# A recurrent step whose candidate's input v and candidate n lie in spare PSUM columns instead of SBUF

## The chip, the cores and the metric

One core of a Trainium2 chip runs the kernel. The time is that of one execution on the device, in microseconds (us); the profile is one execution taken by the hardware profiler. Engines: PE multiplies matrices (PEld is its weight load), DVE is the vector engine, ACT the scalar engine with tanh, POOL and SP have side roles here. SBUF is the working memory, PSUM the memory that PE writes its products to; DVE and ACT can read it, too.

## The reference

Four layers follow each other, each between two layer norms and added to its input x of 8 sequences, 512 tokens and 128 features. The first layer is a gated recurrent unit (GRU) with 256 hidden values, and only this one matters here. It goes through the 512 tokens one after the other:

```python
def step(h, xt):
    xr_t, xz_t, xn_t = xt
    r = jax.nn.sigmoid(xr_t + h @ w_hr.T + b_hr)
    z = jax.nn.sigmoid(xz_t + h @ w_hz.T + b_hz)
    n = jnp.tanh(xn_t + r * (h @ w_hn.T + b_hn))
    h_new = (1.0 - z) * n + z * h
    return (h_new, h_new)
```

The other three are a feed-forward layer with experts, an attention layer and a second feed-forward layer.

## The kernel before

The hidden state of all 8 sequences is kept turned: 128 partitions hold half of the 256 hidden values, and 16 columns (NSTEP) are the 2 halves times 8 sequences. So every elementwise operation of a step works on a tile of 128x16. For the matmuls the state is split into a high and a low fp16 part, the tile GB.

The 512 steps are written as 32 groups of 16 steps. The function `schedule` writes out, for each engine, the order: `steps` is the recurrent step itself, and between two steps `inputs`, `early`, `late` and `prepare` place pieces of other work (the layer norm of coming tokens, the output product of the GRU, the expert layer, weights for later stages). Each engine has one queue and takes its instructions in the order in which they are written; `wait_ge` on a semaphore holds the queue until another instruction has counted it up.

One step is, in the names of the code and the lines of the profile:

- PE (L731) multiplies the state by the recurrent weights, in the order r, part of n, rest of r, rest of n, z: 36 matmuls of 128x8. `r_ps`, `hn_tr` and `z_ps` are counted up as r, n and z are complete. Then it adds the input products and biases of the next four steps (`inject`, L739 and L744).
- ACT takes tanh of the r gate from PSUM: tr (L935).
- DVE makes u = (tr + 1) * hn with the product hn from PSUM (L1027), and v = u + xn with the input part xn from PSUM (L1031).
- ACT takes tanh of the z gate: tz (L937), and then tanh of v: n (L939).
- DVE makes zg = (tz + 1) * h (L1034), and zn = (tz - 1) * n (L1037). zg stands ahead of zn in DVE's queue.
- DVE makes the new state 0.5 * zg - zn, once as the high part in GB (L1041) and once in f32 in HR (L1042), and the low part as their difference (L1044). PE waits for the high part before the next step's first matmul, and for the low part a little later.

The sigmoids are written as tanh of half the argument, with factors folded into the weights.

PSUM has 8 banks of 512 f32 columns for each partition. Banks 0 and 1 belong to the r gate (pR), 2 and 3 to z (pZ), 4 and 5 to the candidate (pN), two banks each because four steps (U = 4) use bank p while the next four are prepared in bank 1 - p. In a pN bank the columns 0 to 63 hold hn and 64 to 127 hold xn of four steps; the columns from 128 on (2 * U * NSTEP) are not used. tr, tz, u_, v_, n_, zg and zn lie in SBUF.

Of the kernel before, what the change touches and what calls it, by code (L numbers as in the profile page):

```python
# [21 lines left out]
ALU = mybir.AluOpType  # L22
ACT = mybir.ActivationFunctionType
AX = mybir.AxisListType

P = 128
# [12 lines left out]
U = 4  # L39
NSTEP = HC * B  # L40
# [20 lines left out]
def build(nc, x_d, gamma_d, beta_d, w_ih_d, w_hh_d, b_ih_d, b_hh_d, w_out_d, b_out_d,  # L61
# [4 lines left out]
    with top:  # L66
        def sb(ctx, name, shape, dt=F32):
            return ctx.enter_context(nc.sbuf_tensor(name, shape, dt))
# [46 lines left out]
        def signal(name, per=1, credit=0):  # L115
            return Signal(top.enter_context(nc.semaphore(name)), per, credit)
# [83 lines left out]
        ctx = ExitStack()  # L200
# [251 lines left out]
        ctx = ExitStack()  # L452
        with ctx:
# [7 lines left out]
            tr = sb(ctx, "tr", [P, NSTEP])  # L461
            tz = sb(ctx, "tz", [P, NSTEP])
            u_ = sb(ctx, "u_", [P, NSTEP])
            v_ = sb(ctx, "v_", [P, NSTEP])
            n_ = sb(ctx, "n_", [P, NSTEP])
            zg = sb(ctx, "zg", [P, NSTEP])
            zn = sb(ctx, "zn", [P, NSTEP])
            warm = sb(ctx, "warm2", [P, 1])
            pR = PS[:, 0:2, :]
            pZ = PS[:, 2:4, :]  # L470
            pN = PS[:, 4:6, :]

            hr_start = signal("hr_start")
            x_stats = Signal(stats.sem, 1, 2)
# [23 lines left out]
            v_ready = signal("v_ready")  # L498
            n_ready = signal("n_ready")
            zg_ready = signal("zg_ready")  # L500
            zn_ready = signal("zn_ready")
# [419 lines left out]
            def _(act):  # L921
# [3 lines left out]
                n_scale = act.alloc_register("n_scale")  # L925
# [3 lines left out]
                def steps(first, s, ring):  # L929
                    p, k = s // U % 2, s % U  # L930
                    n = first + (s + 1) if isinstance(first, int) else act.snap(first + (s + 1))
                    now = lambda bank: bank[:, p, 0:U * NSTEP].rearrange("p (c u b) -> p c u b", c=HC, u=U)[:, :, k, :]
                    as_states = lambda x: x[:, :].rearrange("p (c b) -> p c b", c=HC)
                    act.wait_ge(r_ps.sem, n)
                    act.activation(as_states(tr), now(pR), ACT.Tanh, scale=gate_scale).then_inc(hn_tr.sem, 1)  # L935
                    act.wait_ge(z_ps.sem, n)
                    act.activation(as_states(tz), now(pZ), ACT.Tanh, scale=gate_scale).then_inc(tz_ready.sem, 1)  # L937
                    act.wait_ge(v_ready.sem, n)
                    act.activation(n_[:, :], v_[:, :], ACT.Tanh, scale=n_scale).then_inc(n_ready.sem, 1)  # L939

                def inputs(j, s):
                    if s == 0:
# [20 lines left out]
                def prepare(a):  # L963
# [38 lines left out]
                    if a == 7 * GS + 3:  # L1002
                        act.wait_ge(wsc.sem, wsc.value(act, 0, 8))
                        act.activation(WH[:, :], wguT[:, :], ACT.Copy, scale=W_UP).then_inc(wsplit.sem, 1)
                schedule(act, steps, inputs, early, late, prepare)

            @block.vector
            def _(dve):
# [8 lines left out]
                def steps(first, s, ring):  # L1017
                    p, k = s // U % 2, s % U
                    n = first + (s + 1) if isinstance(first, int) else dve.snap(first + (s + 1))
                    n2 = (first + (s + 1)) * 2 if isinstance(first, int) else dve.snap(first * 2 + 2 * (s + 1))  # L1020
                    by_chunk = lambda x: x.rearrange("p (c b) -> p c b", c=HC)
                    hn, xn = [pN[:, p, i * U * NSTEP:(i + 1) * U * NSTEP].rearrange("p (c u b) -> p c u b", c=HC, u=U)[:, :, k, :]
                              for i in range(2)]
                    before, now = HR[:, 1 - s % 2, :], HR[:, s % 2, :]

                    dve.wait_ge(hn_tr.sem, n2)
                    dve.scalar_tensor_tensor(by_chunk(u_[:, :]), by_chunk(tr[:, :]), 1.0, hn,  # L1027
                                             ALU.add, ALU.mult).then_inc(u_ready.sem, 1)

                    dve.wait_ge(u_ready.sem, n)  # L1030
                    dve.tensor_tensor(by_chunk(v_[:, :]), by_chunk(u_[:, :]), xn, ALU.add).then_inc(v_ready.sem, 1)  # L1031

                    dve.wait_ge(tz_ready.sem, n)
                    dve.scalar_tensor_tensor(zg[:, :], tz[:, :], 1.0, before, ALU.add, ALU.mult).then_inc(zg_ready.sem, 1)  # L1034

                    dve.wait_ge(n_ready.sem, n)
                    dve.scalar_tensor_tensor(zn[:, :], tz[:, :], 1.0, n_[:, :], ALU.subtract, ALU.mult).then_inc(zn_ready.sem, 1)  # L1037

                    dve.wait_ge(zn_ready.sem, n)
                    high, low = [GB[:, ring, i, :, s, :] for i in range(2)]  # L1040
                    dve.scalar_tensor_tensor(high, by_chunk(zg[:, :]), 0.5, by_chunk(zn[:, :]), ALU.mult, ALU.subtract).then_inc(g1_ready.sem, 1)  # L1041
                    dve.scalar_tensor_tensor(now, zg[:, :], 0.5, zn[:, :], ALU.mult, ALU.subtract).then_inc(g_ready.sem, 1)  # L1042
                    dve.wait_ge(g_ready.sem, n)
                    dve.tensor_tensor(low, by_chunk(now), high, ALU.subtract).then_inc(g2_ready.sem, 1)  # L1044
# [102 lines left out]
                def prepare(a):  # L1147
# [106 lines left out]
                    if a in (7 * GS + 5, 7 * GS + 10):  # L1254
                        half_w = slice(0, HID) if a == 7 * GS + 5 else slice(HID, 2 * HID)
                        dve.wait_ge(wsplit.sem, wsplit.value(dve, 0, 1))
                        dve.wait_ge(wsc.sem, wsc.value(dve, 0, 8))
                        dve.scalar_tensor_tensor(WL[:, half_w], wguT[:, half_w], W_UP, WH[:, half_w], ALU.mult, ALU.subtract).then_inc(wsplit.sem, 1)
                schedule(dve, steps, inputs, early, late, prepare)

        def layer_norm_scale(eng, mv, rt, rs, step, b, k):
# [23 lines left out]
        ctx = ExitStack()  # L1285
        with ctx:
# [61 lines left out]
            xn = signal("xn_ready", NT)  # L1348
# [1196 lines left out]
```

## Time and profile before

| | |
|---|---|
| median of 3 runs | 1646.24 us |
| the runs | 1638.33 to 1646.63 us |
| span of the profiled execution, first to last instruction | 1636.9 us |
| the profiled execution's own time with what lies around the span | not listed |
| the recurrence in it (25 to 1019 us) | 994 us |
| what follows (1019 to 1636.9 us) | 618 us |
| busy over the span: PE, DVE, ACT | 1365.0, 1143.2, 704.4 us |

A share of busy time tells little here. A step is a chain through three engines that repeats 512 times, so the thing to read is the order of time within one step: when each instruction starts, how long it takes, and which of its two inputs came last. An instruction of DVE or ACT is shown with its start and its duration; the time between the end of one and the start of the one that waits for it is the cost of handing over.

### The profile page before, as it was taken

What the parts mean: (1) busy time and instruction counts of PE and PEld (TensorE: products, weight loads), DVE (VectorE), ACT (ScalarE), POOL (GpSimd) and SP (SyncE); (2) the same over time, 40 slices, a digit from 0 to 9 for tenths busy, and PEclk for the clock granted to TensorE, in tenths of its full rate; (3) what the DMA queues carried; (4) which work ended last, traced back from release to release, by engine and by line L of the source; (5) the groups of instructions that cost most, each with busy time, mean ns of one, the idle gap of its engine ahead of it and who ended that gap; (6) DMA issues with size and microseconds to landing.
All of it is one profiled execution on the core that took longest, in us unless ns stands there. A gap on an engine that the chain in (4) does not pass through costs nothing. (4 is left out here: it accounts for less than half of the span.)

```text
span 1636.9 us, 65673 instructions
## 1 busy us (share of the span) xinstructions
PE 1365.0 (83%) x27355; PEld 1027.9 (63%) x27370; DVE 1143.2 (70%) x5594; ACT 704.4 (43%) x2475; POOL 434.8 (27%) x818
## 2 busy tenths in 40 slices
PE   5888888878878888888888887379999999999886
PEld 4667777767767777777777776245556555555443
DVE  5767777777777777777777776557576776776485
ACT  3333223222222222222222222136777777777765
POOL 2001111111111111111111111364245535522354
PEclk6555555555555555555555555578999999999998
DMA  5200000000000000000000000068537735742001
GB/s 120 29 4 5 5 7 5 5 6 5 5 5 7 5 5 6 5 5 7 5 5 7 5 5 7 7 140 139 73 66 110 98 58 89 106 68 29 1 14 39
DMA packets 68941, 53.70 MB, mean 33 GB/s; under 512 B 12686, under 2 KB 68390, under 8 KB 68646
## 3 DMA queue, kind: packets, MB, share of 16 engines
q1 hardware_dynamic: 66470, 49.32, 18.3%
q8 instruction: 215, 3.52, 0.9%
q14 instruction: 80, 0.66, 0.1%
q10 hardware_dynamic: 2176, 0.20, 0.1%
HBM read 31.84 MB, written 15.47 MB: 29 GB/s over the span
## 5 line engine op out<-in xcount | busy, mean ns | idle before, releaser
L731 PE MATMUL PS<-GB,W 128*128 128x8 f16 x18432 | 575.7, 168 | 177.3 <-DVE GB L1041 173.2
L731 PEld LDWEIGHTS PS<-GB,W 128*128 128x128 f16 x18432 | 532.6, 104 | 285.9 <-DVE GB L1041 281.1
L935 ACT ACTIVATE tr<-PS 128x16 f32<-128x16 f32 x512 | 94.7, 185 | 490.2 <-PE PS L731 490.2
L2383 DVE TENSOR_REDUCE MX<-PS 128x1 f32<-128x512 f32 (+3 forms) x352 | 220.0, 635 | 114.8 <-PE PS L1842 111.6
L2121 ACT ACTIVATE PT<-PS 128x512 f32<-128x512 f32 (+1 forms) x352 | 193.2, 566 | 114.7 <-PE PS L1858 110.1
L937 ACT ACTIVATE tz<-PS 128x16 f32<-128x16 f32 x512 | 94.2, 184 | 192.0 <-PE PS L731 192.0
L1027 DVE SCALAR_TENSOR_TENSOR u_<-tr,PS 128x16 f32<-128x16 f32 x512 | 87.4, 171 | 126.0 <-PE PS L731 114.0
L685 POOL TENSOR_TENSOR rt<-mv,eps 128x1 f32<-128x1 f32 x96 | 18.4, 191 | 553.1 <-DVE mv L1052 553.1
L1034 DVE SCALAR_TENSOR_TENSOR zg<-tz,HR 128x16 f32<-128x16 f32 x512 | 90.1, 176 | 81.5 <-ACT tz L937 81.4
L1839 PE MATMUL PS<-KS,QS 99*128 99x256 bf16 (+3 forms) x512 | 134.0, 314 | 12.8 <-DVE MX L2383 8.5
L1855 PE MATMUL PS<-QS,KS 102*128 102x256 bf16 (+3 forms) x512 | 128.8, 302 | 6.2 <-ACT PT L2121 5.6
L744 PE MATMUL PS<-Y,V 128*128 128x32 f16 x2322 | 130.9, 188 | 0.0
L739 PE MATMUL PS<-ones,brow 128*128 128x32 bf16 x1032 | 110.3, 188 | 2.1 <-PEq L201 2.1
L939 ACT ACTIVATE n_<-v_ 128x16 f32<-128x16 f32 x512 | 110.5, 216 | 0.4 <-DVE v_ L1031 0.2
L1044 DVE TENSOR_TENSOR GB<-HR,GB 128x16 f16<-128x16 f32 x512 | 89.5, 175 | 17.4
L1041 DVE SCALAR_TENSOR_TENSOR GB<-zg,zn 128x16 f16<-128x16 f32 x512 | 89.3, 174 | 17.6
L1031 DVE TENSOR_TENSOR v_<-u_,PS 128x16 f32<-128x16 f32 x512 | 87.1, 170 | 17.5
L744 PEld LDWEIGHTS PS<-Y,V 128*128 128x128 f16 x2322 | 98.7, 104 | 0.0
L1839 PEld LDWEIGHTS PS<-KS,QS 99*128 99x128 bf16 x512 | 45.0, 102 | 78.6 <-DVE MX L2383 37.4
L1037 DVE SCALAR_TENSOR_TENSOR zn<-tz,n_ 128x16 f32<-128x16 f32 x512 | 89.6, 175 | 0.6 <-ACT n_ L939 0.2
L1842 PE MATMUL PS<-maskU,identb 128*128 128x128 bf16 x512 | 89.5, 226 | 0.0
L1858 PE MATMUL PS<-maskL,identb 128*128 128x128 bf16 x512 | 86.9, 220 | 0.0
(393 smaller groups left out, 2496.8 us busy)
## 6 DMA issues: line engine op xcount, KB each, us to landing
QS<-q_parts SPq DMA_DIRECT2D x90, 128.0 KB, 11.0
KS<-k_parts SPq DMA_DIRECT2D x90, 128.0 KB, 13.1
q_parts<-PQ SPq DMA_DIRECT2D x16, 384.0 KB, 10.4
k_parts<-PK SPq DMA_DIRECT2D x16, 384.0 KB, 3.3
X<-XM SPq DMA_DIRECT2D x32, 64.0 KB
out_dram<-X SPq DMA_DIRECT2D x8, 256.0 KB, 2.3
XM<-in_L_attn_x_dram SPq DMA_DIRECT2D x16, 80.0 KB
s_hh<-in_L_attn_w_hh_dram SPq DMA_DIRECT2D x1, 768.0 KB, 5.4
```

The lines of the kernel that those rows point to most:

```text
L731: return pe.matmul(bank[:, p, at:at + B], W[:, kc, w:w + P], state[:, part, kc, :], start=False, stop=True, skip_group_check=True)
L739: pe.matmul(o, brow[:, (bias + mc) * P:(bias + mc + 1) * P], ones3[:, :], start=start and mc == 0, stop=False, skip_group_check=True)
L744: pe.matmul(o, V[:, w], Y[:, rows], start=False, stop=False, skip_group_check=True)
L935: act.activation(as_states(tr), now(pR), ACT.Tanh, scale=gate_scale).then_inc(hn_tr.sem, 1)
L937: act.activation(as_states(tz), now(pZ), ACT.Tanh, scale=gate_scale).then_inc(tz_ready.sem, 1)
L939: act.activation(n_[:, :], v_[:, :], ACT.Tanh, scale=n_scale).then_inc(n_ready.sem, 1)
L1034: dve.scalar_tensor_tensor(zg[:, :], tz[:, :], 1.0, before, ALU.add, ALU.mult).then_inc(zg_ready.sem, 1)
L1037: dve.scalar_tensor_tensor(zn[:, :], tz[:, :], 1.0, n_[:, :], ALU.subtract, ALU.mult).then_inc(zn_ready.sem, 1)
L1839: pe.matmul(bank[:, a * w:(a + 1) * w], QS[0:KM, p, 4 * g + i, q], KS[0:KM, p, 4 * g + i, 0:w], start=(a == 0), stop=False, skip_group_che ...
L1855: pe.matmul(bank[:, a * w:(a + 1) * w], KS[0:KF, p, 4 * g + i, j * P:(j + 1) * P], QS[0:KF, p, 4 * g + i, j * P:S], start=(a == 0), stop=F ...
L2121: act.activation(PT_OF[j][:, heads[0]:heads[-1] + 1, :], p_e[:, k % 2, 0:len(heads) * w].rearrange("p (a w) -> p a w", w=w), ACT.Exp).then ...
L2383: dve.tensor_reduce(MX[:, g % 2, heads[0]:heads[-1] + 1, NT - 1 - it], p_x[:, k % 2, 0:len(heads) * w].rearrange("p (a w) -> p a w", w=w), ...
```

## The change

v and n get new places. Instead of two SBUF tiles of 128x16 they are views of the candidate gate's own PSUM bank, the one of the current p: v in columns 128 to 143, n in columns 144 to 159. DVE writes v to PSUM (it already reads xn from the same bank), ACT reads v from PSUM and writes n to PSUM, and DVE reads n from PSUM for zn. No instruction, wait or semaphore is added, removed or moved.

```diff
-            v_ = sb(ctx, "v_", [P, NSTEP])
-            n_ = sb(ctx, "n_", [P, NSTEP])
...
+            def v_of(p):
+                return pN[:, p, 2 * U * NSTEP:2 * U * NSTEP + NSTEP]
+
+            def n_of(p):
+                return pN[:, p, 2 * U * NSTEP + NSTEP:2 * U * NSTEP + 2 * NSTEP]
...
-                    act.activation(n_[:, :], v_[:, :], ACT.Tanh, scale=n_scale).then_inc(n_ready.sem, 1)
+                    act.activation(n_of(p), v_of(p), ACT.Tanh, scale=n_scale).then_inc(n_ready.sem, 1)
...
-                    dve.tensor_tensor(by_chunk(v_[:, :]), by_chunk(u_[:, :]), xn, ALU.add).then_inc(v_ready.sem, 1)
+                    dve.tensor_tensor(by_chunk(v_of(p)), by_chunk(u_[:, :]), xn, ALU.add).then_inc(v_ready.sem, 1)
...
-                    dve.scalar_tensor_tensor(zn[:, :], tz[:, :], 1.0, n_[:, :], ALU.subtract, ALU.mult).then_inc(zn_ready.sem, 1)
+                    dve.scalar_tensor_tensor(zn[:, :], tz[:, :], 1.0, n_of(p), ALU.subtract, ALU.mult).then_inc(zn_ready.sem, 1)
```

## Rows read from the trace of the kernel before

**Rows 1.** Stage totals: stretch, length, busy us (instructions) per engine, PE clock, DMA.
```profile
25.00:1019.00 994.00, 816.15 (x22962) 705.15 (x22959) 723.65 (x4497) 297.78 (x1679) 157.42 (x364) 0.50 0.04 9
1019.00:1636.90 617.90, 540.58 (x4316) 316.04 (x4331) 406.82 (x1061) 399.37 (x785) 270.93 (x425) 0.92 0.43 69
```
**Rows 2.** Groups, 60 to 1090 us: busy us, mean ns | idle before, releasers.
```profile
L731 PE MATMUL PS<-GB,W 128*128 128x8 f16 x17776 | 555.2, 168 | 170.7 <-DVE GB L1041 166.7
...
L939 ACT ACTIVATE n_<-v_ 128x16 f32<-128x16 f32 x494 | 106.6, 216 | 0.4 <-DVE v_ L1031 0.2
...
L935 ACT ACTIVATE tr<-PS 128x16 f32<-128x16 f32 x494 | 91.4, 185 | 474.4 <-PE PS L731 474.4
L937 ACT ACTIVATE tz<-PS 128x16 f32<-128x16 f32 x494 | 90.9, 184 | 185.2 <-PE PS L731 185.2
...
L1037 DVE SCALAR_TENSOR_TENSOR zn<-tz,n_ 128x16 f32<-128x16 f32 x494 | 86.5, 175 | 0.6 <-ACT n_ L939 0.2
...
L1027 DVE SCALAR_TENSOR_TENSOR u_<-tr,PS 128x16 f32<-128x16 f32 x494 | 84.4, 171 | 118.5 <-PE PS L731 106.6
L1031 DVE TENSOR_TENSOR v_<-u_,PS 128x16 f32<-128x16 f32 x494 | 84.1, 170 | 16.9
```
**Rows 3.** Order of time, one step: start us, duration us, instruction [idle before, releaser].
```profile
600.37 0.18 ACT L935 ACTIVATE tr<-PS 128x16 f32<-128x16 f32 x1 [1.08 <-PE PS L731]
600.61 0.17 DVE L1027 SCALAR_TENSOR_TENSOR u_<-tr,PS 128x16 f32<-128x16 f32 x1 [0.17 <-PE PS L731]
...
600.82 0.17 DVE L1031 TENSOR_TENSOR v_<-u_,PS 128x16 f32<-128x16 f32 x1
...
600.93 0.18 ACT L937 ACTIVATE tz<-PS 128x16 f32<-128x16 f32 x1 [0.38 <-PE PS L731]
...
601.02 0.22 ACT L939 ACTIVATE n_<-v_ 128x16 f32<-128x16 f32 x1
...
601.15 0.18 DVE L1034 SCALAR_TENSOR_TENSOR zg<-tz,HR 128x16 f32<-128x16 f32 x1 [0.16 <-ACT tz L937]
601.27 0.18 DVE L1037 SCALAR_TENSOR_TENSOR zn<-tz,n_ 128x16 f32<-128x16 f32 x1
601.48 0.17 DVE L1041 SCALAR_TENSOR_TENSOR GB<-zg,zn 128x16 f16<-128x16 f32 x1
601.58 0.17 DVE L1042 SCALAR_TENSOR_TENSOR HR<-zg,zn 128x16 f32<-128x16 f32 x1
...
601.71 1.04 PE L731 MATMUL PS<-GB,W 128*128 128x8 f16 x33 [0.26 <-DVE GB L1041]
...
602.31 0.18 ACT L935 ACTIVATE tr<-PS 128x16 f32<-128x16 f32 x1 [1.07 <-PE PS L731]
```
**Rows 4.** Order of time on DVE, end of the last of the 155 steps.
```profile
899.91 0.17 DVE L1034 SCALAR_TENSOR_TENSOR zg<-tz,HR 128x16 f32<-128x16 f32 x1 [0.16 <-ACT tz L937]
900.03 0.17 DVE L1037 SCALAR_TENSOR_TENSOR zn<-tz,n_ 128x16 f32<-128x16 f32 x1
900.24 0.17 DVE L1041 SCALAR_TENSOR_TENSOR GB<-zg,zn 128x16 f16<-128x16 f32 x1
900.33 0.17 DVE L1042 SCALAR_TENSOR_TENSOR HR<-zg,zn 128x16 f32<-128x16 f32 x1
```
**Rows 5.** Order of time, a step in which DVE had other work before u.
```profile
255.57 0.17 DVE L1031 TENSOR_TENSOR v_<-u_,PS 128x16 f32<-128x16 f32 x1
255.74 0.18 DVE L1034 SCALAR_TENSOR_TENSOR zg<-tz,HR 128x16 f32<-128x16 f32 x1
255.78 0.21 ACT L939 ACTIVATE n_<-v_ 128x16 f32<-128x16 f32 x1
...
256.03 0.18 DVE L1037 SCALAR_TENSOR_TENSOR zn<-tz,n_ 128x16 f32<-128x16 f32 x1
```
**Rows 6.** Order of time on PE, a step with much other work.
```profile
605.20 0.31 PE L856 MATMUL PS<-DN,IL 128*128 128x128 f16 x1
...
605.59 0.27 PE L731 MATMUL PS<-GB,W 128*128 128x8 f16 x4
```

## The prediction

> **What bounds the kernel now.** I read the stage totals first, then the groups of instructions, then one recurrent step in order of time. The stage totals cut the span in two: 994 us of recurrence, 512 steps one after the other, and 618 us that the diff doesn't touch [rows 1]. Inside the recurrence PE is busy for 816 of the 994 us, DVE for 724 and ACT for 298: none is at its limit, so look for a chain of latencies. 994 / 512 is 1.94 us a step, and in the groups each link of the step has the same count [rows 2].
>
> The step in order of time gives the chain [rows 3]. Read from tr: tr starts at 600.37, u at 600.61, v at 600.82, n at 601.02, zn at 601.27, the state GB at 601.48. PE starts the next step's matmuls at 601.71, and the next tr starts at 602.31. The steps agree with each other to the last digit shown. I read the 155 steps between 600 and 900 us the same way; the first is that of [rows 3], the end of the last stands in [rows 4]. Their mean spacings are tr to u 0.241, u to v 0.207, v to n 0.203, n to zn 0.249, zn to GB 0.210, and from GB to the next tr 0.83: 1.94 us. So everything from v to zn is on the path today, and 1 ns taken from each step is 0.512 us of the kernel.
>
> A second branch runs beside it: PE finishes the z gate, ACT makes tz (600.93), DVE makes zg (601.15), and zg stands ahead of zn in DVE's queue. Two rows off the pattern show which branch releases zn. At 255 us a busy DVE made u and v late, with tz long done: n still follows v by 0.21 and zn follows n by 0.25, while zg was 0.29 ahead [rows 5]. So n releases zn. But in the usual step zg is only 0.12 ahead, and the only pair of SBUF operations here that run back to back, GB and HR, start 0.09 to 0.10 apart [rows 3, 4]. Over the 155 steps the means are 0.1206 and 0.0915: zn can move up by 0.029 us and no more, whatever happens to n. Then PE's z gate, ACT's tz and zg set the step.
>
> **The change part by part.** No instruction, wait, semaphore or DMA is added or taken away, and no queue is reordered. Three instructions per step change the memory of an operand: v (DVE) writes PSUM, n (ACT) reads and writes PSUM, zn (DVE) reads n from PSUM. u, tr, tz, zg, GB, HR and the low part stay.
>
> *n reads PSUM.* Same operation, same shape, same SBUF output: tr and tz read PSUM and take 185 and 184 ns, n reads SBUF and takes 216 [rows 2]. I take the whole difference: -31 ns.
>
> *zn reads PSUM.* By duration there is nothing to pay: u and v, with one PSUM input, take 171 and 170 ns, zn, all SBUF, 175 [rows 2]. By start after a wait on DVE's own result: v (reads PSUM) starts 0.207 - 0.171 = 0.036 after u's end, GB (reads SBUF) 0.210 - 0.175 = 0.035 after zn's end. That is +1 ns. A dearer reading exists: u starts 0.241 - 0.185 = 0.056 after tr's end, zg only 0.218 - 0.184 = 0.034 after tz's end, and u reads PSUM. If PSUM is the cause, zn pays +22 ns. The view of groups puts most of u's idle time down to PE (the hn product that u also needs), not to tr [rows 2], so I take +1 and keep +22 as the upper bound. Below, -5 (the difference of durations).
>
> *v writes PSUM; n writes PSUM.* No row of this trace has DVE or ACT writing PSUM. Both write 128x16 f32, as before. The largest difference between the two memories that any row shows for this size is the 31 ns above, so I bound each by -31 and +31. A saving on v would be worth little: n would then stand behind tz, which starts only 0.09 ahead of it [rows 3]. I take 0 for both: on DVE the nearest rows (PSUM reads) differ from SBUF by 5 ns at most; for ACT the only known sign is a gain, which the room at zg would swallow anyway.
>
> VectorE: DVE Perf Modes, a page of the Trainium skill, section "The TRN2 errata", speaks against this change: it gives VectorE 58 cycles of fixed cost from SBUF and 120 from PSUM at 0.96 GHz, and ScalarE 224 and 172 at 1.2 GHz. My estimate from that page would be +65 ns for zn and -43 for n, +22 a step, 11 us slower. This trace bears out the ScalarE half in sign (31 ns) and not the VectorE half (171 and 170 against 175).
>
> *What is hidden.* PE's other work, after the z gate, must be done by the time GB releases the next step. PE's idle time there is 170.7 us over 17776 matmuls, 36 to a step, so 0.35 us on average [rows 2]; in a tight step the filler's last matmul ends at 605.51 and the next step's first starts at 605.59 [rows 6], so 0.03 us less still fits. I counted 62 of 477 steps with under 0.11 us of it; should each of those lose 0.03, that is 2 us. DVE's side work lies between the low part and the next u, a stretch that starts with GB and doesn't shrink. While v and n are in use PE writes the z gate's banks and injects into the candidate's other bank (1 - p), so it has no need to wait for them.
>
> *The sum.* -31 (n's read) + 1 (zn's read) + 0 + 0 = -30 ns against a room of 29: -29 ns x 512 = -14.8 us. The profiled execution spans 1636.9 us; what lies around the span isn't shown, but it is 1.4 us under the fastest run (1638.3) and 9.3 under the median (1646.2). The saving is per step and holds for either; the runs shown themselves spread by 0.5%. From the median: 1646.2 - 14.8 = **1631.4 us**; from the span it would be 1622.1 plus what lies around it.
>
> **The rivals.**
>
> *VectorE pays for PSUM (slower).* DVE's write-back of v and its read of n are both dearer than to SBUF, by the two upper bounds: +31 and +22, less n's 31: +22 ns a step, +11.3 us, **1657.5 us**. It decides for slower (by 0.5%, 8.2 us, 16 ns a step) as soon as DVE's two PSUM accesses together cost more than 47 ns. For it: nothing here shows a DVE write to PSUM, and u starts late. Against it: the two DVE groups that read PSUM take no longer than the one that doesn't [rows 2]. The errata section of the Trainium skill's page VectorE: DVE Perf Modes, named above, comes out at nearly the same time.
>
> *One price only (no change).* Only zn's read costs 22: -9 ns, -4.6 us, 1641.6. Or only v's write costs 31: 0, 1646.2. Either eats the gain, and the edit is a wash. For it: u's late start. Against it: PE as the shown cause.
>
> *The room is smaller.* zn, reading PSUM, may not start 0.0915 behind zg but later; every 10 ns costs 5.1 us of the gain. The case of no change begins at 13 ns.
>
> *More than the room (faster).* Nothing on this path can give more than 29 ns unless PE runs faster. PE's granted clock is 0.50 (the 1.2 GHz level) through the recurrence and 0.92 after it [rows 1]; an idle stretch shorter by 0.03 of 0.35 us gives me no reason to expect another level. If it came, the z branch would shorten too.
>
> **How the numbers follow.** Forecast, with a gain of 16 to 29 ns: 0.55. More than that: 0.02. One price or a smaller room, within 8 us: 0.23. VectorE pays: 0.20. A difference of 0.5% (1638.0 or 1654.5 us) is about what a measurement of this kernel can tell from no change, so faster 0.57, same 0.23, slower 0.20. The unknown costs reach from -29 ns (1631.4) to +31 - 31 + 31 + 22 = +53 ns (+27.1 us, 1673.4). The forecast's own range is 1620 to 1638: the low end is the fastest run less 14.8, 1623.5, and a little for spread. The range of 8 in 10 runs from 1620 to 1659: it holds the case of no change and half of the slower one; what lies above, some 0.1, is v's write and n's write both dear.
>
> **What would show it.** Right: n, now PS<-PS, at about 185 ns or less; v at 170; zn starting about 0.09 after zg; DVE idle before zn no longer ended by n; a step of 1.91 us. Wrong: v well over 200 ns; zn starting later than 0.25 after n; a spacing zg to zn at 0.12 or more. If n falls to 185 and the step stays at 1.94, look at v's duration and at n's start after v first. The 618 us after the recurrence should be the same; if they differ, that isn't this change.

## The result, and the profile after

The changed kernel took 1626.0 us (median of 4 runs, 1624.6 to 1630.5) against 1646.4 (4 runs): a ratio of 0.9886, 95% interval 0.9862 to 0.991. By the ratio it is faster by 1.1%, 18.8 us of 1646.4 (the two medians lie 20.4 apart), where 14.8 were forecast. The profiled execution spans 1624.5 us.

The stage totals of the changed kernel, in the columns of [rows 1], cut at 1000 us, where the recurrence now ends:
```profile
25.00:1000.00 975.00, 816.51 (x22960) 705.45 (x22957) 709.27 (x4495) 277.26 (x1679) 155.32 (x364) 0.50 0.04 9
1000.00:1624.50 624.50, 546.30 (x4316) 321.68 (x4331) 407.26 (x1062) 399.23 (x785) 270.78 (x425) 0.92 0.43 68
```
The whole gain is in the recurrence. The exact cut is the first and the last tr of the 512 steps; this is the view of one line (duration shortest/median/longest, first and last start), for the kernel before:
```profile
L935 ACT ACTIVATE tr<-PS x512: 185/185/185, 24.9 to 1017.7; 128x16 f32<-128x16 f32 x171
```
and for the changed one, whose lines stand 4 lower from here on:
```profile
L939 ACT ACTIVATE tr<-PS x512: 183/183/183, 24.9 to 999.0; 128x16 f32<-128x16 f32 x171
```
992.8 us became 974.1: 18.7 us less, 37 ns for each of 511 steps. The usual step went from 1.94 to 1.90 us.

The groups of the changed kernel, as in [rows 2]:
```profile
L939 ACT ACTIVATE tr<-PS 128x16 f32<-128x16 f32 x494 | 90.4, 183 | 471.4 <-PE PS L735 471.3
L941 ACT ACTIVATE tz<-PS 128x16 f32<-128x16 f32 x494 | 90.4, 183 | 187.0 <-PE PS L735 187.0
L1035 DVE TENSOR_TENSOR PS<-u_,PS 128x16 f32<-128x16 f32 x494 | 88.1, 178 | 16.9
...
L1045 DVE SCALAR_TENSOR_TENSOR GB<-zg,zn 128x16 f16<-128x16 f32 x494 | 86.3, 175 | 16.8
...
L943 ACT ACTIVATE PS<-PS 128x16 f32<-128x16 f32 x494 | 83.0, 168 | 0.4 <-DVE PS L1035 0.2
L1041 DVE SCALAR_TENSOR_TENSOR zn<-tz,PS 128x16 f32<-128x16 f32 x494 | 81.2, 164 | 0.4 <-ACT PS L943 0.2
```
v (now `PS<-u_,PS`) went from 170 to 178 ns, n (`PS<-PS`) from 216 to 168, zn (`zn<-tz,PS`) from 175 to 164. Nothing else in the step changed by more than 2 ns.

One step of the changed kernel in order of time, to be laid beside [rows 3]:
```profile
601.39 0.18 ACT L939 ACTIVATE tr<-PS 128x16 f32<-128x16 f32 x1 [1.07 <-PE PS L735]
...
601.83 0.18 DVE L1035 TENSOR_TENSOR PS<-u_,PS 128x16 f32<-128x16 f32 x1
...
601.95 0.18 ACT L941 ACTIVATE tz<-PS 128x16 f32<-128x16 f32 x1 [0.38 <-PE PS L735]
...
602.04 0.17 ACT L943 ACTIVATE PS<-PS 128x16 f32<-128x16 f32 x1
602.16 0.18 DVE L1038 SCALAR_TENSOR_TENSOR zg<-tz,HR 128x16 f32<-128x16 f32 x1 [0.15 <-ACT tz L941]
602.25 0.16 DVE L1041 SCALAR_TENSOR_TENSOR zn<-tz,PS 128x16 f32<-128x16 f32 x1
602.45 0.17 DVE L1045 SCALAR_TENSOR_TENSOR GB<-zg,zn 128x16 f16<-128x16 f32 x1
602.54 0.17 DVE L1046 SCALAR_TENSOR_TENSOR HR<-zg,zn 128x16 f32<-128x16 f32 x1
602.68 0.81 PEld L735 LDWEIGHTS PS<-GB,W 128*128 128x128 f16 x27 [0.75 <-DVE GB L1045]
```
zn stands 0.09 behind zg, as HR stands behind GB: the two run back to back. Over 158 steps between 600 and 900 us, of which this is the first, the means, in the trace's own nanoseconds, are tr to v 0.445 us (0.446 before), v to n 0.213 (0.204), n to zn 0.209 (0.248), zg to zn 0.092 (0.121), zn to GB 0.198 (0.210). From tr to GB that is 1.066 us for 1.107. The rest, GB to the next tr, is 0.835 for 0.833.

### The profile page after: what moved, and what is told of

The parts are those of the page before. It is cut to its first block and busy times, and to the rows that moved or that the text cites. A ratio compares the mean times of both kernels' runs of the same rounds, so it can differ in the third digit from the quotient of the medians.

```text
span 1624.5 us, 65673 instructions
## 1 busy us (share of the span) xinstructions
PE 1371.2 (84%) x27355; PEld 1033.9 (64%) x27370; DVE 1129.3 (70%) x5594; ACT 683.8 (42%) x2475; POOL 432.6 (27%) x818
## 3 DMA queue, kind: packets, MB, share of 16 engines
q1 hardware_dynamic: 66470, 49.32, 18.8%
## 5 line engine op out<-in xcount | busy, mean ns | idle before, releaser
L1035 DVE TENSOR_TENSOR PS<-u_,PS 128x16 f32<-128x16 f32 x512 | 91.3, 178 | 17.5
L1048 DVE TENSOR_TENSOR GB<-HR,GB 128x16 f16<-128x16 f32 x512 | 90.2, 176 | 17.4
L1045 DVE SCALAR_TENSOR_TENSOR GB<-zg,zn 128x16 f16<-128x16 f32 x512 | 90.0, 176 | 17.4
L943 ACT ACTIVATE PS<-PS 128x16 f32<-128x16 f32 x512 | 86.0, 168 | 0.4 <-DVE PS L1035 0.2
L1046 DVE SCALAR_TENSOR_TENSOR HR<-zg,zn 128x16 f32<-128x16 f32 x512 | 86.1, 168 | 0.0
```

Source lines behind the costliest of these rows:

```text
L1035: dve.tensor_tensor(by_chunk(v_of(p)), by_chunk(u_[:, :]), xn, ALU.add).then_inc(v_ready.sem, 1)
```

## The experiments

The step times below are means over the steps between 590 and 910 us, the durations means between 600 and 900 us; "the 512 steps" are counted from the first tr to the last. The theory after the result: each operand's memory has a price of its own on the operation; n's prices are the large ones; and z's branch (PE, tz, zg) now sets zn's start, with n ready only a little earlier. Each edit is shown against the changed kernel, shortened.

**v alone in PSUM.**
```diff
-  act.activation(n_of(p), v_of(p), ...)
+  act.activation(n_[:, :], v_of(p), ...)
-  dve.scalar_tensor_tensor(zn[:, :], tz[:, :], 1.0, n_of(p), ...)
+  dve.scalar_tensor_tensor(zn[:, :], tz[:, :], 1.0, n_[:, :], ...)
```


> v in PSUM, n back in SBUF. Theory (each operand has its own price): v stays at 178 ns (170 in SBUF), n reads PSUM and writes SBUF and takes 185 as tr and tz do (216 before, 168 after), zn reads SBUF and takes 175 again. From tr, n ends at 0.844 us and zn starts 0.03 later at 0.876, which is 0.10 after zg, so n is still the later one. The step is 1.915 us (1.939 before, 1.900 after), 12 us of the 512 steps. Rival (n's 48 ns come from its write alone): n takes 216, v costs 8 more, the step is 1.948 us, 4 us slower than before.

Its groups:
```profile
L944 ACT ACTIVATE n_<-PS 128x16 f32<-128x16 f32 x157 | 28.9, 184 | 0.0
...
L1036 DVE TENSOR_TENSOR PS<-u_,PS 128x16 f32<-128x16 f32 x156 | 27.8, 179 | 5.3
...
L1042 DVE SCALAR_TENSOR_TENSOR zn<-tz,n_ 128x16 f32<-128x16 f32 x157 | 27.4, 174 | 0.0
```
The step is 1.917 us, the ratio 0.9945 (0.9929 to 0.996). The theory's numbers stand, the rival is out: reading v from PSUM takes 32 ns off n, writing v there adds 8 to v. zn starts 0.098 us after zg, so n releases it. Against the changed kernel the step is 16 ns longer, and most of that is two things: zn starts 7 ns later, and it takes 174 ns and not 164.

**n alone in PSUM.**
```diff
-  act.activation(n_of(p), v_of(p), ...)
+  act.activation(n_of(p), v_[:, :], ...)
-  dve.tensor_tensor(by_chunk(v_of(p)), ...)
+  dve.tensor_tensor(by_chunk(v_[:, :]), ...)
```


> n in PSUM, v back in SBUF. Theory (each operand has its own price): v takes 170, n reads SBUF and writes PSUM and takes about 200 (216 less the 16 that the write saves), zn reads PSUM and takes 164. zn starts 0.88 after tr, 0.105 after zg, and the state follows 0.198 later: a step of 1.912 us, 14 us less than before in the 512 steps. Rival (the write alone is what makes n short): n takes 168, zn stands 0.09 behind zg, the step is 1.900 as with both. Second rival (zn's shorter time has another cause than its PSUM input): zn takes 175.

Its groups:
```profile
L944 ACT ACTIVATE PS<-v_ 128x16 f32<-128x16 f32 x157 | 29.4, 187 | 0.0
...
L1042 DVE SCALAR_TENSOR_TENSOR zn<-tz,PS 128x16 f32<-128x16 f32 x157 | 26.8, 170 | 0.0
L1036 DVE TENSOR_TENSOR v_<-u_,PS 128x16 f32<-128x16 f32 x157 | 26.8, 170 | 5.4
```
The step is 1.908 us, the ratio 0.9919 (0.9887 to 0.9951): a little better than forecast. The write to PSUM takes 29 ns off n by itself, not 16. So the two savings don't add up: 32 and 29 alone, 48 together. And zn takes 170 here, neither the 164 of the theory nor the 175 of the second rival, though it reads the same operand as in the changed kernel.

**v in another bank.**
```diff
 def v_of(p):
-    return pN[:, p, 2 * U * NSTEP:2 * U * NSTEP + NSTEP]
+    return pR[:, p, 2 * U * NSTEP:2 * U * NSTEP + NSTEP]
```


> As the changed kernel, but v in the spare columns of the r gate's bank, so that v doesn't read and write one bank, nor n. Theory (v's 8 ns more are the price of a write to PSUM): v 178, n 168, step 1.900 us. Rival (one bank for reading and writing costs something): v 170 or n below 168. By the theory that zg sets zn's start the step stays at 1.900 either way, with zn 0.091 behind zg; if n set it, 8 ns off v would give 1.892.

The group of v:
```profile
L1035 DVE TENSOR_TENSOR PS<-u_,PS 128x16 f32<-128x16 f32 x158 | 28.2, 179 | 5.4
```
v took 179 ns, n 168, zn 164, the step 1.901 us (one run, 1622.6 us). Reading and writing one bank costs nothing here: v's 8 ns are the price of the write. As v's duration didn't move, the run doesn't tell what sets zn.

**zn ahead of zg.**
```diff
+  dve.wait_ge(n_ready.sem, n)
   dve.wait_ge(tz_ready.sem, n)
-  dve.scalar_tensor_tensor(zg[:, :], tz[:, :], 1.0, before, ...)
-  dve.wait_ge(n_ready.sem, n)
   dve.scalar_tensor_tensor(zn[:, :], tz[:, :], 1.0, n_of(p), ...)
-  dve.wait_ge(zn_ready.sem, n)
+  dve.scalar_tensor_tensor(zg[:, :], tz[:, :], 1.0, before, ...)
+  dve.wait_ge(zg_ready.sem, n)
```


> As the changed kernel, but DVE takes zn before zg and the state waits for zg. Shows when n would release zn by itself. Theory (zg sets zn's start in the changed kernel, n is some 9 ns ahead): zn starts 0.200 after n's start in place of 0.210. zg then starts 0.09 behind zn and the state 0.21 behind zg: a step of 1.99 us, 48 us slower than the changed kernel over the 512 steps. Rival (n still sets zn's start): 0.210 as before, the step 2.00 us.

Its groups:
```profile
L1039 DVE SCALAR_TENSOR_TENSOR zn<-tz,PS 128x16 f32<-128x16 f32 x151 | 25.7, 170 | 35.7 <-ACT PS L943 35.7
...
L1040 DVE SCALAR_TENSOR_TENSOR zg<-tz,HR 128x16 f32<-128x16 f32 x151 | 25.5, 169 | 0.0
```
In the usual step zn starts 0.200 after n, not 0.210, and its idle time is now ended by n: left to itself, n would release zn some 10 ns earlier than zg lets it start. So zg sets zn's start in the changed kernel, by a small margin. The step is 1.987 us (one run, 1670.2 us). These rows also bear on zn's duration. zn released by n takes 170 here as in the run with n alone in PSUM, and zg, which now starts straight behind another operation, takes 169 in place of 175.

The changed kernel shows the same without an edit. In five of its 512 steps DVE was late with u and v, among them the step of [rows 5], and zn waits for n long after zg has started:
```profile
252.20 0.18 DVE L1038 SCALAR_TENSOR_TENSOR zg<-tz,HR 128x16 f32<-128x16 f32 x1
252.24 0.17 ACT L943 ACTIVATE PS<-PS 128x16 f32<-128x16 f32 x1
...
252.44 0.17 DVE L1041 SCALAR_TENSOR_TENSOR zn<-tz,PS 128x16 f32<-128x16 f32 x1
```
In these five zn takes 170 to 171 ns, in the usual steps 164. Its end moves less than its start: it ends 0.202 us after n's end where n releases it, in the five steps and in the edited run alike, and 0.206 after it in the usual step of the changed kernel. So zg's place ahead of zn costs 4 ns there, not 10.

**The changed kernel again, and with zg in PSUM, too.** The first is the changed kernel without an edit; both ran beside the same runs of the kernel before.

> The changed kernel once more, for a tighter ratio beside the next kernel. Theory (some 36 to 39 ns a step are the whole effect): recurrence 974 us from the first tr to the last, ratio 0.988 to 0.989. The part after the recurrence took 619 us before and 619 to 626 in the kernels so far, which share its code; theory: that is scatter, so it lies in that band again, and the rival (the change makes it longer) would give 625 again.

The ratio is 0.9894 (0.9869 to 0.9919), the 512 steps take 973.2 us, the step 1.901. The part after the recurrence took 625.9 us, about the figure of the rival and the upper edge of the theory's band; what this leaves open stands in the next section.

```diff
+  def zg_of(p):
+      return pZ[:, p, U * NSTEP:U * NSTEP + NSTEP]
...
-  dve.scalar_tensor_tensor(zg[:, :], tz[:, :], ...)
+  dve.scalar_tensor_tensor(zg_of(p), tz[:, :], ...)
-  dve.scalar_tensor_tensor(high, by_chunk(zg[:, :]), 0.5, by_chunk(zn[:, :]), ...)
-  dve.scalar_tensor_tensor(now, zg[:, :], 0.5, zn[:, :], ...)
+  dve.scalar_tensor_tensor(high, by_chunk(zg_of(p)), 0.5, by_chunk(zn[:, :]), ...)
+  dve.scalar_tensor_tensor(now, zg_of(p), 0.5, zn[:, :], ...)
```


> As the changed kernel, with zg in spare columns of the z gate's bank, too. Theory (an input from PSUM takes 5 ns off a vector operation that waits for its release, a write to PSUM adds 8 that here lie beside zn): zg 184, zn still 0.09 behind zg, GB 170 in place of 175: step 1.895 us, 2.5 us in all, ratio to before about 0.987. Rival (the whole 11 ns of zn came from its input): GB 164, step 1.889. Rival the other way (a following operation starts later behind one that writes PSUM): zn 0.10 behind zg, step 1.903 or more.

Its groups:
```profile
L1040 DVE SCALAR_TENSOR_TENSOR PS<-tz,HR 128x16 f32<-128x16 f32 x158 | 29.0, 184 | 24.1 <-ACT tz L943 20.0
L1047 DVE SCALAR_TENSOR_TENSOR GB<-PS,zn 128x16 f16<-128x16 f32 x158 | 27.6, 175 | 5.4
...
L1048 DVE SCALAR_TENSOR_TENSOR HR<-PS,zn 128x16 f32<-128x16 f32 x158 | 25.9, 164 | 0.0
```
Neither version of the gain came: GB stays at 175 and the step at 1.900 us. zn stands 0.092 behind zg, so the rival the other way is out, too. The ratio to the kernel before is 0.9879 (0.9859 to 0.99), not to be told from the changed kernel's own, so this isn't a better version. The 8 ns that zg's write costs lie beside zn, as expected.

**zn in PSUM, too.**
```diff
-  dve.scalar_tensor_tensor(zn[:, :], tz[:, :], 1.0, n_of(p), ...)
+  dve.scalar_tensor_tensor(zn_of(p), tz[:, :], 1.0, n_of(p), ...)
-  dve.scalar_tensor_tensor(high, by_chunk(zg[:, :]), 0.5, by_chunk(zn[:, :]), ...)
-  dve.scalar_tensor_tensor(now, zg[:, :], 0.5, zn[:, :], ...)
+  dve.scalar_tensor_tensor(high, by_chunk(zg[:, :]), 0.5, by_chunk(zn_of(p)), ...)
+  dve.scalar_tensor_tensor(now, zg[:, :], 0.5, zn_of(p), ...)
```


> As the changed kernel, with zn written to the z gate's bank, too. Theory: zn 164 + 8 = 172, GB 170, step 1.903 us: what the read gives the write takes. Rival (GB gets 11 ns shorter): step 1.897.

Its groups:
```profile
L1043 DVE SCALAR_TENSOR_TENSOR PS<-tz,PS 128x16 f32<-128x16 f32 x158 | 27.1, 171 | 0.0
...
L1047 DVE SCALAR_TENSOR_TENSOR GB<-zg,PS 128x16 f16<-128x16 f32 x158 | 26.9, 170 | 5.4
...
L1048 DVE SCALAR_TENSOR_TENSOR HR<-zg,PS 128x16 f32<-128x16 f32 x157 | 25.6, 163 | 0.0
```
As the theory has it: the write adds 7 to zn, the read takes 4 to 5 off GB, the step is 1.901 us (one run, 1623.8 us). Here GB gets shorter by its PSUM input, where in the run before it didn't. What differs for GB is the place of the operand: there it was the first input, here the second. But HR, which reads the same two operands straight behind GB, gets shorter from either place, 164 and 163 ns for 168. So the place alone doesn't explain it, and the cause stays open.

**v and tz in PSUM, n in SBUF.**
```diff
-  act.activation(as_states(tz), now(pZ), ...)
+  act.activation(as_states(tz_of(p)), now(pZ), ...)
-  act.activation(n_of(p), v_of(p), ...)
+  act.activation(n_[:, :], v_of(p), ...)
-  dve.scalar_tensor_tensor(zg[:, :], tz[:, :], 1.0, before, ...)
-  dve.scalar_tensor_tensor(zn[:, :], tz[:, :], 1.0, n_of(p), ...)
+  dve.scalar_tensor_tensor(zg[:, :], tz_of(p), 1.0, before, ...)
+  dve.scalar_tensor_tensor(zn[:, :], tz_of(p), 1.0, n_[:, :], ...)
```


> [...] Makes the z branch shorter and n longer than in the changed kernel. Theory (n is last again): tz 168, n 184, zg at 0.761 after tr, zn at 0.875 and 0.114 behind zg, zn 170 as it waits for n and reads PSUM: step 1.913 us. Rival (the z branch sets the step whatever n does): 1.886.

Its groups:
```profile
L1044 DVE SCALAR_TENSOR_TENSOR zn<-PS,n_ 128x16 f32<-128x16 f32 x157 | 27.4, 174 | 0.0
L1041 DVE SCALAR_TENSOR_TENSOR zg<-PS,HR 128x16 f32<-128x16 f32 x157 | 27.3, 174 | 21.4
...
L944 ACT ACTIVATE PS<-PS 128x16 f32<-128x16 f32 x156 | 26.2, 168 | 58.8 <-PE PS L738 58.8
```
tz (`PS<-PS`) takes 168, zg starts 0.200 after tz in place of 0.215, and zn stands 0.114 behind zg: n is last again. The step is 1.917 us (one run, 1631.3 us), the same as with v alone in PSUM and 4 ns over the forecast's 1.913, because zn, with PSUM as its first input, takes 174 and not 170. The later of the two branches decides; a shorter z branch alone doesn't help.

## Why the prediction was right

It said faster, by 14.8 us; measured were 18.8 by the ratio and 18.7 in the recurrence of the two traces. Point by point:

- **The chain.** Right. v, n, zn and GB lay on the path, and what they lost is the gain. From tr to GB the usual step lost 41 ns: 30 up to zn's start and 11 from there to GB. GB to the next tr gave 2 back; why, the runs don't tell.
- **n reads PSUM, -31.** Right: -32 where it stands alone.
- **n writes PSUM, taken as 0.** Wrong in size, inside the bounds: -29 alone, -16 on top of the read. The prediction held that the room at zg would swallow a gain here. It didn't: with v alone in PSUM, so without this write, the step is 1.917 us and not 1.901.
- **v writes PSUM, taken as 0.** +8, inside the bounds. There is luck in the sum here: n's read less v's write are 23 ns, as the run with v alone in PSUM measured, and not the 29 that fill the room. Only the other term that was taken as 0, n's write, filled it.
- **The room of 29 ns.** Right, and it was used up: zn moved from 0.121 to 0.092 behind zg. n starts 9 ns later and is 48 shorter, so it ends 39 earlier, and the run with zn ahead of zg shows the 10 that zn can't use as slack at its start.
- **zn's read, +1.** This term was mis-sized: zn got 11 ns shorter, outside the bounds of -5 to +22. Over 512 steps 11 ns are 5.6 us, more than the 4 us by which the sum fell short. The +1 itself came from starts rounded to 0.01 us; unrounded, u to v and zn to GB hand over in 34 ns each. Two parts make up the 11. A PSUM second input takes 5 ns off (170 against 175, in the two runs and the five steps of the changed kernel in which n releases zn). The other 6 come from standing in the queue: zn no longer waits for n but starts straight behind zg, and an operation that does so was shorter in each case here (zn 164 for 170; zg, put behind zn, 169 for 175). The sum left out that taking a wait away can also shorten the operation that waited.
- **VectorE pays for PSUM, 0.20.** It doesn't: +8 for the write, no more for a read. The errata section of VectorE: DVE Perf Modes (the Trainium skill), by which reading PSUM costs VectorE 62 cycles more, isn't borne out by any row here: writing to SBUF, its operations of this size take 163 to 175 ns with a PSUM input and 167 to 177 without one. Nor does a PSUM input delay the start, as u's late start might have meant: n to zn, now from PSUM, takes n's duration and 0.032 us (0.200 - 0.168 with zn ahead of zg), as it took from SBUF (0.248 - 0.216). That leaves PE for u's late start, as the releasers had it.
- **PE's other work.** Right: GB to PE's first matmul stays at 0.23 us (602.45 to 602.68).
- **The part after the recurrence.** From the last tr to the end it took 619.2 us before and 625.5 after, so the span lost only 12.4. In the other profiled kernels, which all share its code, it took 618.8 to 625.9: 620.3 and 618.8 with one operand moved, 621.2 with v in another bank, 625.2 with the slow order, 625.9 and 624.0 in the repeated pair, 623.9 in the last two runs. I take it as scatter, but these single traces don't rule out that the change adds a little: the kernels with both v and n in PSUM took 621.2 to 625.9, the others 618.8 to 623.9. The ratios bound it: they give 18.8 us and, in the repetition, 1.06% or 17.4 us, where the recurrences of the profiled runs lost 18.7 and 19.7. That leaves 0 to 2 us of the 6, within the intervals. And the unchanged kernel, beside the repetition, itself ran in 1638.9 to 1645.7 us. The cause stays open. PE's granted clock falls below 1.00 at other places in each of the two traces, as in these two stretches of the changed one; 19 us later, where the kernel before does the same work, it had 1.00:
```profile
1099.30:1149.30 50.00, 48.63 (x404) 28.93 (x404) 30.09 (x63) 35.92 (x72) 18.53 (x30) 0.93 0.50 77
...
1299.30:1399.30 100.00, 95.38 (x809) 57.99 (x814) 68.16 (x174) 71.44 (x142) 40.22 (x63) 0.97 0.51 76
```

## What to carry to other kernels

In a chain of small operations that hands over from engine to engine, a small tile that ACT reads or writes can be worth a place in PSUM: for the 128x16 f32 tanh here some 30 ns an operation for either side, 48 for both, at a price of 8 ns for a DVE write. Before counting such a gain, look for the branch beside it: the distance of the waiting operation from the one ahead of it in its queue, less the distance of two that run back to back, is all that its start can move. Then look at its end, too: the operation, freed of its wait, can get shorter itself.

## What the runs showed of the hardware

A 128x16 f32 tanh on ACT takes 216 ns from SBUF to SBUF, 184 from PSUM to SBUF, 187 from SBUF to PSUM and 168 from PSUM to PSUM: the second saving is only half the first. A DVE operation of this size that waits for its release takes 170 to 171 ns with PSUM as its second input, 174 to 175 with PSUM as its first, and 174 to 176 with SBUF alone. Straight behind another operation of its queue zn and zg took 6 ns less. Writing to PSUM adds 7 to 8.

The clock row of one run misleads. The stage total of the run with zn in PSUM has 1.00 (the 2.4 GHz level) through the recurrence, against 0.50 (1.2 GHz) in the other profiled runs:
```profile
25.00:1000.00 975.00, 815.38 (x22961) 704.31 (x22958) 708.98 (x4500) 277.77 (x1679) 156.01 (x364) 1.00 0.04 9
```
But the trace of this run holds no record of the clock before 1050 us, and a stretch without a record is shown as 1.00. Its matmuls speak against it. These are a 128x128 f32 matmul of the changed kernel's recurrence (clock 0.50), the same one in this run's recurrence, and one of the same size later in this run, where the clock is on record as 1.00:
```profile
L792 PE MATMUL PS<-ident,YNp 128*128 128x128 f32 x30 | 13.6, 454 | 0.0
...
L794 PE MATMUL PS<-ident,YNp 128*128 128x128 f32 x30 | 13.6, 454 | 0.0
...
L1928 PE MATMUL PS<-ident,OT 128*128 128x128 f32 x44 | 6.9, 278 | 0.0
```
So this recurrence most likely went at the lower level as well, and its equal step (1.901 us) and equal matmuls of 8 columns,
```profile
L737 PE MATMUL PS<-GB,W 128*128 128x8 f16 x5687 | 177.4, 168 | 48.1 <-DVE GB L1047 42.6
```
don't show what a faster clock would do to the step. No run here shows that.
